# A first stage that loads six tiles of x first and builds its edge tables inside the loop over node tiles

## The chip, the core and the metric

The kernel runs on one core of one Trainium2 chip. The metric is the device time of one execution in microseconds (us). A core has TensorE (PE; its weight loads are shown as PEld), VectorE (DVE), ScalarE (ACT), GpSimd (POOL) and SyncE (SP), and 16 DMA engines that serve the queues of SP, ACT and POOL.

## The reference, cut to what matters

Two rounds of a relational graph layer and a mixture-of-experts layer, with 6250 nodes of 256 features and 100000 edges that are sorted by destination. The change touches only what feeds the first graph layer:

```python
x = x + _L0_gnn_ref(_layernorm(x, axis=-1), L0_gnn_W, L0_gnn_attn_src, L0_gnn_attn_dst, edge_index, edge_type_8)
...
h_all = jnp.einsum('nf,rof->rno', x, W).reshape(r, n, h, d)
src, dst = (edge_index[0], edge_index[1])
h_src = h_all[edge_type, src]
h_dst = h_all[edge_type, dst]
scores = jnp.einsum('ehd,hd->eh', h_src, attn_src) + jnp.einsum('ehd,hd->eh', h_dst, attn_dst)
```

Each node's normalised features are multiplied by 8 relation matrices of 256 x 256 and by the attention vectors folded into them. What follows reads one projected row for each edge.

## The kernel before, in words

The program is a sequence of stages with a barrier between them. The first, `relation_rows` (stage name `rows`), does three things.

**The loop over node tiles.** 6250 nodes are 49 tiles of 128. For each tile VectorE normalises (`Norm.normalise`, L228), TensorE transposes two blocks into PSUM (`Norm.transpose`, L236), ScalarE copies them to SBUF (`Norm.keep`, L265), TensorE multiplies by the 8 matrices (`product`, L643, into four PSUM banks in turn) and by the 64 columns for the destination half (L648), ScalarE copies the 8 results into one of two buffers `hb` (L470), VectorE copies the destination half (`half`, L543), and SP stores the buffer to `h_tab` in HBM (L424). VectorE normalises two tiles ahead; its order in the loop is normalise t+2, copy half t, then whatever table work is put behind tile t (`turns_at`). So what it does behind tile t stands ahead of the normalisation of tile t+3, which TensorE transposes after product t+1.

**What must come before the loop.** The matrices `wn` are loaded (SP, L405) and transposed by 32 matmuls (L616), ScalarE copies them (L451), and 64 small matmuls multiply them by the attention vectors (L623), which sit word by word in `ablk` (16 DMAs, L411). The mean and variance of all 49 tiles are made by `tile_stats` (L201, four quarters of x as ACT's queue loads them, L447 and L448) and `statistics`; ScalarE takes one square root of all variances (`root`, L222), for which it loads a table.

**The tables of edges.** Edges are cut into groups of 256 that never cross a block of 128 destination nodes. The destination of the first edge of each run of 128 (781 words, L401) is stored to HBM and loaded to 49 partitions (L407); VectorE counts positions (L492), GpSimd gathers a window of 256 edges for each block (L361), VectorE counts the cuts and groups (L504 to L510), TensorE makes prefix sums and spreads them (L628, L630), VectorE finds for each group its block, first edge and length (L520 to L533), and GpSimd gathers the rows and destinations of all groups, 8 indirect DMAs (L365, L367). The rest of it (`turn0` to `turn3`, `keep`, `turn5`, GpSimd's masks) already runs inside the loop, behind tiles 4 to 30.

The order of the work is written out by hand: each engine's program is a list, and semaphores tie them. The tables of edges stand ahead of the loop in VectorE's and TensorE's lists, and between the first and the second quarter of the statistics. SP waits in its list for the list of first edges (`first_st`) ahead of the attention vectors, and for the group table (`at_ok`) ahead of the loop's stores.

```python
            pe.wait_ge(consts, 1)
            pe.wait_ge(weights, 16 * 17)
...
            pe.wait_ge(need_ok, 1)
...
            turns_at = {4: turn0, 6: turn1, 8: turn2, 10: turn3, 30: turn5}
```

## Time and profile before

| | us |
|---|---|
| median of 3 runs | 3263.57 |
| lowest and highest run | 3260.66, 3266.58 |
| the profiled execution's own time | 3259.22 |
| its span, first to last instruction | 3257.2 |
| PE busy | 2189.7 (67% of the span) |
| DVE, ACT, POOL busy | 1780.9, 1332.3, 1589.4 |

The profile is one execution, taken by the hardware profiler. "Busy" counts the time in which an engine has an instruction under way; matmuls are pipelined, so a busy PE is not PE at its peak. PEclk is the granted TensorE clock as a share of full speed: 1.00 is 2.4 GHz, 0.50 is 1.2 GHz. SPq and ACTq are the issues of DMAs by SP and ACT; the duration of such a row is the time that the issuing engine spent on it, not that of the transfer. A releaser in brackets is what ended the idle time before an instruction.

### The profile page before, as it was taken

The page shows a single profiled execution, that of the slowest core. Times are in us where ns is not written, and L with a number is a line of the kernel's source. Part 1 is how long each engine was busy: PE and PEld are TensorE (multiplying, and loading weights), DVE is VectorE, ACT ScalarE, POOL GpSimd, SP SyncE. Part 2 cuts the span into 40 slices and gives each one's busy share as a digit, 9 for nine tenths or more (in the row PEclk, how much of TensorE's full clock was granted, in tenths as well). Part 3 has the DMA queues.
Part 4 walks back from the last instruction along what each step waited for, and adds up shares of the span by engine and source line. Part 5 has one row for each costly group of instructions (what it writes and reads, how often), then busy time and mean ns, then how long its engine had stood idle before and what let it go on. Part 6 is the DMA issues. An engine that isn't in the chain of part 4 may idle for free. (4 is left out here: it accounts for less than half of the span.)

```text
span 3257.2 us, 51141 instructions
## 1 busy us (share of the span) xinstructions
PE 2189.7 (67%) x13091; PEld 1849.9 (57%) x13092; DVE 1780.9 (55%) x4102; ACT 1332.3 (41%) x2969; POOL 1589.4 (49%) x1585
## 2 busy tenths in 40 slices
PE   2999985777777777777626085350430079999998
PEld 1888874656666556565426074230430069999997
DVE  4111125777777777776675434426663365656564
ACT  0444444655565655555301053130111344444443
POOL 1056217777777777777250534327227223334333
PEclk8999986888888888888755588685555589999999
DMA  6355447777765555556542244222302632222221
GB/s 141 126 208 213 193 172 210 214 209 211 208 194 144 145 145 145 144 144 132 53 123 72 78 158 144 68 74 51 97 31 104 210 77 42 46 48 47 48 47 26
DMA packets 225887, 402.34 MB, mean 124 GB/s; under 512 B 58684, under 2 KB 153543, under 8 KB 219086
## 3 DMA queue, kind: packets, MB, share of 16 engines
q0 software_dynamic: 84864, 206.63, 26.2%
q1 hardware_dynamic: 122002, 187.73, 17.3%
q10 hardware_dynamic: 18892, 6.45, 0.9%
q8 instruction: 57, 0.93, 0.1%
q14 instruction: 72, 0.59, 0.1%
HBM read 247.26 MB, written 155.68 MB: 124 GB/s over the span
## 5 line engine op out<-in xcount | busy, mean ns | idle before, releaser
L720 POOL DMA_INDIRECT sum_ring<-h_tab,gnn_edge_row x880 | 839.4, 954 | 268.0 <-issue 260.7
L981 PE MATMUL sum_bank<-sum_ring,sum_one_hot 128*128 128x264 f32 x1760 | 583.0, 494 | 215.2 <-issue 195.7
L981 PEld LDWEIGHTS sum_bank<-sum_ring,sum_one_hot 128*128 128x128 f32 x1760 | 418.7, 247 | 334.5 <-issue 227.0
L1802 POOL DMA_INDIRECT out_dram<-moe_y,moe_to_node x112 | 185.9, 1659 | 383.9 <-ACT moe_y L1828 353.0
L643 PE MATMUL rows_bank<-rows_w_rows,rows_xnT 128*128 128x264 f32 x1568 | 358.6, 387 | 1.7 <-ACT rows_xnT L265 1.7
L643 PEld LDWEIGHTS rows_bank<-rows_w_rows,rows_xnT 128*128 128x128 f32 x1568 | 295.1, 191 | 50.3 <-ACT rows_xnT L265 2.1
L770 ACT ACTIVATE sum_distance_by_lane<-all_iota,gnn_minus_local 128x128 bf16<-128x128 f32 x880 | 267.3, 386 | 0.1
L836 DVE TENSOR_TENSOR sum_ring<-sum_ring,sum_bank 128x1024 f32<-128x1024 f32 x220 | 265.7, 1209 | 0.5 <-ACT sum_ring L784 0.4
L970 PEld LDWEIGHTS sum_bank<-gnn_dst_half,sum_one_hot_T 128*128 128x128 f32 x1760 | 226.2, 205 | 43.9 <-issue 40.3
L970 PE MATMUL sum_bank<-gnn_dst_half,sum_one_hot_T 128*128 x1760 | 230.9, 289 | 28.7 <-ACT sum_one_hot_T L763 14.3
L1960 PE MATMUL moe_bank<-moe_w_low,moe_hidden_high 128*128 x896 | 244.2, 273 | 0.0
L1960 PE MATMUL moe_bank<-moe_w_high,moe_hidden_high 128*128 x896 | 244.2, 273 | 0.0
L1960 PE MATMUL moe_bank<-moe_w_high,moe_hidden_low 128*128 x896 | 244.2, 273 | 0.0
L470 ACT ACTIVATE rows_h_rows<-rows_bank 128x264 f32<-128x264 f32 x392 | 152.9, 390 | 198.5 <-PE rows_bank L643 198.5
L843 DVE TENSOR_TENSOR nodes_acc<-sum_bank,nodes_acc 128x264 f32 x440 | 188.2, 428 | 47.7 <-PE sum_bank L981 19.3
L1844 ACT ACTIVATE moe_hidden<-moe_bank,moe_b_T 128x256 f32<-128x256 f32 x456 | 186.3, 475 | 42.8 <-PE moe_bank L1950 25.5
L543 DVE COPY gnn_dst_half<-rows_bank 128x64 f32<-128x64 f32 x49 | 11.0, 225 | 332.1 <-PE rows_bank L648 332.1
L775 ACT ACTIVATE sum_one_hot<-sum_distance_by_lane,all_ones 128x1024 f32<-128x1024 bf16 x110 | 126.3, 1148 | 147.4 <-PE sum_bank L981 145.5
L1950 PE MATMUL moe_bank<-moe_x_high,moe_w_high 128*128 128x256 f16 x912 | 175.3, 274 | 1.7 <-DVE moe_x_low L1894 1.7
L1950 PE MATMUL moe_bank<-moe_x_low,moe_w_high 128*128 128x256 f16 x912 | 175.3, 274 | 0.0
L1950 PE MATMUL moe_bank<-moe_x_high,moe_w_low 128*128 128x256 f16 x912 | 175.1, 274 | 0.0
L826 DVE TENSOR_TENSOR sum_score<-sum_dst_part,sum_ring 128x64 f32<-128x64 f32 x110 | 24.9, 226 | 266.6 <-DMA sum_ring<-h_tab,gnn_edge_row 266.0
(406 smaller groups left out, 4151.3 us busy)
## 6 DMA issues: line engine op xcount, KB each, us to landing
h_tab<-rows_h_rows SPq DMA_DIRECT2D x49, 1056.0 KB, 3.9
sum_local_rows<-local_tab SPq DMA_DIRECT2D x110, 256.0 KB, 3.8
sorted<-sum_blank_row SPq DMA_DIRECT2D x49, 387.0 KB
moe_stage<-in_L_ffn_W_dram SPq DMA_DIRECT2D x16, 1024.0 KB
moe_tile<-sorted POOLq DMA_DIRECT2D x58, 258.0 KB, 4.1
sum_ring<-h_tab,gnn_edge_row POOLq DMA_INDIRECT x880
sorted<-sum_zero SPq DMA_DIRECT2D x49, 256.0 KB
mask_tab<-rows_masks POOLq DMA_DIRECT2D x7, 1560.0 KB, 7.9
```

The source lines that it names most:

```text
L470: nc.scalar.activation(hb[:, t % 2, r, :], bank[2 + r % 4][:, 0:W0], ACT.Copy).then_inc(h_ok.sem, 1)
L643: last = nc.tensor.matmul(bank[2 + r % 4][:, 0:W0], norm.xT[:, u, c * P:(c + 1) * P], wx[:, c, r, :], start=(c == 0), stop=(c == DC - 1))
L720: nc.gpsimd.indirect_dma_start(ring[:, t % (RING * ST), :], None, k.h_tab, bass.IndirectOffsetOnAxis(k.edge_row[:, t:t + 1], 0)).then_inc( ...
L770: last = nc.scalar.activation(off[:, u * P:(u + 1) * P], k.iota[:, :], ACT.Abs, bias=k.minus_local[:, m * ST + u:m * ST + u + 1])
L836: nc.vector.tensor_tensor(to, to, by, ALU.mult).then_inc(msg_ok, 1)
L843: nc.vector.tensor_tensor(col(k.acc, b), sum_b[g % SG][:, 0:W0], col(k.acc, b), ALU.add).then_inc(added, 1)
L970: last = nc.tensor.matmul(pick_b[n % 2][:, u * R * H0:(u + 1) * R * H0], hotT[:, n % 2, u, :], col(k.dst_half, b[u // G]), start=True, sto ...
L981: last = nc.tensor.matmul(sum_b[j][:, 0:W0], hot[:, m % 2, t, :], ring[:, m % RING * ST + t, :], start=(u == 0), stop=(u == G - 1))
L1802: nc.gpsimd.indirect_dma_start(a["out"], bass.IndirectOffsetOnAxis(to_node[:, n % 2, h:h + 1], 0), y[:, n % 2, h, :], None, bounds_check=N ...
L1844: last = nc.scalar.activation(hg[:, q, m * B1:(m + 1) * B1], bank[q][:, m * B1:(m + 1) * B1], ACT.Gelu, scale=1.0 / (XS * WS), bias=col(b1 ...
L1950: last = nc.tensor.matmul(bank[q][:, m * B1:(m + 1) * B1], w1[pw][:, c, bass.ds(e * F1 + (2 * q + m) * P, P)], xh[px][:, u, c, :], start=( ...
L1960: last = nc.tensor.matmul(bank[6 + u][:, h * D:(h + 1) * D], hh[ph][:, u, m, h * P:(h + 1) * P], w2[pw][:, m, bass.ds(e * D, D)], start=(m ...
```

## The change

It rewrites the first stage's order and leaves every other stage alone.

- **Loads.** SP issues the 8 source vectors, the matrices in two halves, tiles 6 to 17 of x, the 781 first words, the edge columns, then behind the wait for the words the rest of x. ACT issues the 8 destination vectors and tiles 0 to 5 of x. TensorE waits for each half of the matrices on its own, and for the vectors only ahead of the small matmuls.
- **Statistics in four parts** of 6, 12, 15 and 16 tiles: the first ahead of the loop, the others inside (`stats`, `variance`, `scales`; ScalarE's `root` ahead of tiles 3, 10 and 16). `tile_stats` had a loop in the instruction stream, `stats` is written out.
- **The tables of edges** become functions that VectorE runs behind tiles 1, 2, 3, 5 and 7; the two matmuls stand behind tiles 4 and 6; `turn0` to `turn3` move from tiles 4, 6, 8, 10 to 9, 11, 13, 15, the transposed arrays from 13 to 18, `turn5` from 30 to 32, and SP's stores and loads of tables with them.
- **First edges of each node.** Two loads to 128 partitions, one word a time, on ACT's queue ahead of the loop, become two loads of rows on SP behind tile 4, a cast, two transposes on TensorE behind tile 27 and two copies.

```diff
-        NF, TURN0 = E // P, 13
+        NF, TURN0 = E // P, 18
...
+        weights = [s.sem(f"weights_loaded{j}") for j in range(2)]
+        quarter = [0, 6, 18, 33, NT]
...
+            vectors(sp, 0, "L0_gnn_attn_src")
+            for j in range(2):
+                sp.dma_start(wn[:, j * R // 2:(j + 1) * R // 2], a["L0_gnn_W"][j * R // 2:(j + 1) * R // 2].rearrange("r (c p) f -> p r c f", p=P)).then_inc(weights[j], 16)
...
+                load_x(1)
                 sp.dma_start(k.first_s.rearrange("(t o) -> t o", o=1), a["dst"][0:NF * P].rearrange("(t p) -> t p", p=P)[:, 0:1]).then_inc(first_st, 16)
+                sp.dma_start(e_row[:, :], a["src"].rearrange("(p e) -> p e", p=EP)).then_inc(edges, 16)
+                sp.dma_start(e_type[:, :], a["edge_type_8"].rearrange("(p e) -> p e", p=EP)).then_inc(edges, 16)
+                sp.dma_start(line(k.dst_s[0:E]), line(a["dst"])).then_inc(line_st, 16)
...
                 sp.wait_ge(first_st, 16)
                 sp.dma_start(first[:, :], line(k.first_s).broadcast_to([NT, NF])).then_inc(first_in, 16)
...
+                load_x(2)
+                load_x(3)
...
                 for t in range(NT):
                     sp.wait_ge(h_ok.sem, 8 * t + 8 + 4)
                     sp.dma_start(rows(k.h_tab.rearrange("(n r) o -> n (r o)", r=R), t * P, P), flat(hb[:, t % 2, :, :])).then_inc(stored.sems[t % 2], 16)
-                    if t == 11:
+                    if t == 1:
+                        sp.wait_ge(rows_ok, 1)
+                        sp.dma_start(k.row_s[0:E].rearrange("(p e) -> p e", p=EP), e_row[:, :]).then_inc(line_st, 16)
...
+            vectors(act, 1, "L0_gnn_attn_dst")
+            act.dma_start(k.x[:, 0:quarter[1], :], a["x"][0:quarter[1] * P, :].rearrange("(t p) f -> p t f", p=P)).then_inc(loaded[0], 16)
...
-            norm.root(act)
+            root(0)
+            norm.t_ok.start(act)
...
+                if t in (3, 10, 16):
+                    root((3, 10, 16).index(t) + 1)
...
+            stats(0)
+            variance(0)
+            scales(0)
...
-            turns_at = {4: turn0, 6: turn1, 8: turn2, 10: turn3, 30: turn5}
+            turns_at = {1: edge_rows, 2: positions, 3: cuts, 5: block_lines, 7: groups, 9: turn0, 11: turn1, 13: turn2, 15: turn3, 26: first_edges, 28: keep_first, 32: turn5}
+            stats_at = {0: (stats, 1), 1: (variance, 1), 3: (scales, 1), 6: (stats, 2), 8: (variance, 2), 10: (scales, 2),
+                        12: (stats, 3), 14: (variance, 3), 16: (scales, 3)}
...
+                if t in stats_at:
+                    stage, j = stats_at[t]
+                    stage(j)
                 if t in turns_at:
                     turns_at[t]()
...
-            pe.wait_ge(weights, 16 * 17)
             for r in range(R):
+                if r % 4 == 0:
+                    pe.wait_ge(weights[r // 4], 16)
...
+            pe.wait_ge(attn_in, 16 * 2 * H0)
...
+                if t == 4:
+                    pe.wait_ge(need_ok, 1)
+                    nc.tensor.matmul(bank[7][0:NT, 0:1], k.before[0:NT, 0:NT], need[:, :], start=True, stop=True).then_inc(start_ps, 1)
```

The order of SP's DMAs up to the first stores of the loop, before:

```order
L397 DMA rows_edge_rows<-in_src_dram 125x800
L398 DMA rows_edge_type<-in_edge_type_dram 125x800
L399 DMA dst_line<-in_dst_dram 16x6250
L401 DMA first_dst<-in_dst_dram 781x1
L403 DMA row_line<-rows_line_end_i 1x512
L404 DMA dst_line<-rows_line_end_i 1x512
L405 DMA rows_w_natural<-in_L_gnn_W_dram 128x16x256
L407 DMA rows_first_dst<-first_dst 49x781
L411 DMA rows_attn_blocks<-in_L_gnn_attn_src_dram 32x1 x8
L411 DMA rows_attn_blocks<-in_L_gnn_attn_dst_dram 32x1 x8
```

and now:

```order
L355 DMA rows_attn_blocks<-in_L_gnn_attn_src_dram 32x1 x8
L415 DMA rows_w_natural<-in_L_gnn_W_dram 128x8x256 x2
L412 DMA nodes_acc<-in_x_dram 128x12x256
L418 DMA first_dst<-in_dst_dram 781x1
L419 DMA rows_edge_rows<-in_src_dram 125x800
L420 DMA rows_edge_type<-in_edge_type_dram 125x800
L421 DMA dst_line<-in_dst_dram 16x6250
L423 DMA row_line<-rows_line_end_i 1x512
L424 DMA dst_line<-rows_line_end_i 1x512
L426 DMA rows_first_dst<-first_dst 49x781
L412 DMA nodes_acc<-in_x_dram 128x15x256 x2
L430 DMA nodes_acc<-in_x_dram 106x256
```

The weights moved ahead of the edges, and 43 tiles of x (`nodes_acc`) stand on SP, 31 of them behind the load of the first words.

VectorE behind tiles 7, 8 and 9 (L596 is the copy of the destination half, L228 the normalisation of a tile to come), now:

```order
L596 COPY gnn_dst_half<-rows_bank 128x64
L562 TENSOR_SCALAR rows_group<-all_col 128x1 x4
L564 COPY rows_block_lines<-rows_bank 128x147
...
L575 CAST rows_edge_of_group<-rows_of_group 128x4
L228 TENSOR_SCALAR rows_xn<-nodes_acc,rows_mean,rows_rstd 128x256
...
L596 COPY gnn_dst_half<-rows_bank 128x64
L601 TENSOR_SCALAR rows_valid<-rows_lane,rows_of_group 128x256 x4
L602 CAST rows_to_turn<-rows_group_rows 128x1024
L228 TENSOR_SCALAR rows_xn<-nodes_acc,rows_mean,rows_rstd 128x256
```

The first use of the gathered groups (L602) stands two tiles behind the table that the gathers need (L575), and ahead of a tile's normalisation.

ScalarE between the weights and the loop, now:

```order
L476 ACTIVATE rows_w_rows<-rows_bank 128x8x8
L477 ACTIVATE rows_w_dst<-rows_bank 128x64
L481 ACT_TABLE_LOAD
L481 ACTIVATE rows_sd<-rows_var 128x6
L265 ACTIVATE rows_xnT<-rows_bank 128x256 x2
```

The table load and the square root, of 6 columns now, still stand behind the copies of the folded vectors; the two word-by-word loads that stood between square root and L265 are gone.

## Rows read from the trace of the kernel before

**Rows 1.** Busy us by stretch: PE, PEld, DVE, ACT, POOL; PEclk, DMA share, GB/s.
```profile
0.00:82.00 82.00, 16.50 (x104) 15.63 (x105) 36.31 (x131) 8.06 (x17) 15.25 (x23) 0.81 0.61 140
82.00:466.00 384.00, 383.13 (x1882) 331.64 (x1882) 50.49 (x131) 171.52 (x441) 117.95 (x77) 1.00 0.47 177
```

**Rows 2.** Stores of projected rows, whole trace; durations, first and last start.
```profile
L424 SPq DMA_DIRECT2D h_tab<-rows_h_rows x49: 319/320/349, 91.5 to 465.5; - x49
```

**Rows 3.** Time line, 55 to 92 us: start, us, engine, line, operation [idle before].
```profile
55.36 0.15 DVE L520 TENSOR_SCALAR rows_group<-all_col 128x1 f32<-128x1 f32 x1 [0.15 <-DVE rows_diagonal L517]
...
61.47 0.17 DVE L533 CAST rows_edge_of_group<-rows_of_group 128x4 int32<-128x4 f32 x1
...
77.06 0.24 ACT L222 ACTIVATE rows_sd<-rows_var 128x49 f32<-128x49 f32 x1 [21.58 <-DVEq L213]
...
79.01 0.74 DVE L228 TENSOR_SCALAR rows_xn<-nodes_acc,rows_mean,rows_rstd 128x256 f32<-128x256 f32 x2 [0.25 <-DVE rows_rstd L286]
...
81.86 0.66 ACT L265 ACTIVATE rows_xnT<-rows_bank 128x256 f32<-128x256 f32 x2 [4.56 <-issue]
...
82.30 8.79 PE L643 MATMUL rows_bank<-rows_w_rows,rows_xnT 128*128 128x264 f32 x32 [1.70 <-ACT rows_xnT L265]
...
91.54 7.29 PE L643 MATMUL rows_bank<-rows_w_rows,rows_xnT 128*128 128x264 f32 x32
```

**Rows 4.** Time line of 39 to 56 us.
```profile
39.30 6.07 PE L616 MATMUL rows_bank<-all_ident,rows_w_natural 128*128 128x128 f32 x32 [39.30 <-DMA rows_attn_blocks<-in_L_gnn_attn_dst_dram]
...
45.21 8.36 PE L623 MATMUL rows_bank<-rows_attn_blocks,rows_w_natural 128*128 128x16 f32 x64
...
54.20 1.28 ACT L222 ACT_TABLE_LOAD   x1
...
55.32 0.85 PE L630 MATMUL rows_bank<-rows_diagonal,all_ones 49*128 49x147 f32 x2 [1.49 <-DVEq L518]
```

**Rows 5.** Time line of the first 40 us, DMA issues (SPq, ACTq).
```profile
1.29 28.13 ACTq L447 DMA_DIRECT2D nodes_acc<-in_x_dram  x4
...
10.64 0.42 SPq L405 DMA_DIRECT2D rows_w_natural<-in_L_gnn_W_dram  x1
...
22.37 1.30 SPq L407 DMA_DIRECT2D rows_first_dst<-first_dst  x1
23.71 4.12 SPq L411 DMA_DIRECT2D rows_attn_blocks<-in_L_gnn_attn_src_dram  x8
27.87 3.79 SPq L411 DMA_DIRECT2D rows_attn_blocks<-in_L_gnn_attn_dst_dram  x8
29.45 9.93 ACTq L448 DMA_DIRECT2D nodes_acc<-in_x_dram  x1
```

**Rows 6.** Busy time by stretch; last two columns: busy share of DMA, GB/s.
```profile
10.00:20.00 10.00, 0.00 (x0) 0.00 (x0) 1.28 (x3) 0.00 (x0) 0.00 (x0) 1.00 0.84 162
20.00:30.00 10.00, 0.00 (x0) 0.00 (x0) 0.00 (x0) 0.00 (x0) 0.00 (x0) 1.00 1.08 352
```

**Rows 7.** Time line, VectorE and the last mask store of GpSimd.
```profile
62.11 4.01 DVE L201 BATCH_NORM_STATS2 nodes_stats<-nodes_acc  x12 [0.47 <-DVE rows_edge_of_group L533]
...
122.61 1.13 DVE L548 TENSOR_SCALAR rows_valid<-rows_lane,rows_of_group 128x256 f32<-128x256 f32 x4
...
124.38 0.41 DVE L228 TENSOR_SCALAR rows_xn<-nodes_acc,rows_mean,rows_rstd 128x256 f32<-128x256 f32 x1
...
353.30 0.84 POOL L391 DMA_DIRECT2D mask_tab<-rows_masks  x1 [0.30 <-POOL rows_masks L389]
```

**Rows 8.** Busy time by stretch, behind the group gathers.
```profile
74.00:76.00 2.00, 0.00 (x0) 0.00 (x0) 1.87 (x7) 0.00 (x0) 0.00 (x0) 0.50 0.58 204
76.00:78.00 2.00, 0.00 (x0) 0.00 (x0) 1.49 (x6) 0.24 (x1) 0.00 (x0) 0.50 0.00 0
```

**Rows 9.** Busy time by stretch, in the small matmuls; PEclk is third from last.
```profile
50.00:51.00 1.00, 1.00 (x11) 1.00 (x10) 0.29 (x2) 0.00 (x0) 0.00 (x0) 1.00 0.09 16
52.00:53.00 1.00, 1.00 (x7) 1.00 (x6) 0.00 (x0) 0.00 (x0) 0.00 (x0) 0.50 0.00 0
```

More of the change, by code:

```diff
@@ L344, in relation_rows, with vectors @@
         block = s.block()
+        def vectors(eng, j, name):
+            eng.wait_ge(cleared, 1)
+            with nc.allow_non_contiguous_dma(reason="attention vectors, one word a lane"):
+                for h in range(H0):
+                    p0 = h * HD0 % P
+                    eng.dma_start(ablk[p0:p0 + HD0, h * HD0 // P, j * H0 + h:j * H0 + h + 1],
+                                  a[name][h:h + 1, :].rearrange("a b -> b a")).then_inc(attn_in, 16)
         @block.gpsimd
@@ L456, in _, with root @@
                 nc.scalar.activation(wd[:, c, :].rearrange("p (r h) -> p r h", r=R), got_v[:, c, :, 1, :], ACT.Copy).then_inc(v_ok, 1)
-            norm.root(act)
+            def root(j):
+                part = slice(quarter[j], quarter[j + 1])
+                act.wait_ge(norm.var_ok, j + 1)
+                nc.scalar.activation(norm.sd[:, part], norm.var[:, part], ACT.Sqrt).then_inc(norm.sd_ok, 1)
+            root(0)
+            norm.t_ok.start(act)
             h_ok.start(act)
-            with nc.allow_non_contiguous_dma(reason="the first edges, one word a node"):
-                for t, name in ((k.dst_i, "dst"), (k.src_i, "src")):
-                    act.dma_start(t[:, :], a[name][0:NPAD].rearrange("(t p) -> p t", p=P)).then_inc(first_nodes, 16)
             norm.keep(act, 0, 0, d_ps)
             for t in range(NT):
+                if t in (3, 10, 16):
+                    root((3, 10, 16).index(t) + 1)
                 if t + 1 < NT:
@@ L533, in _, with variance @@
-            ch.link(nc.vector.tensor_copy(at_i[:, :], got[:, 1, :]))
-            v.sem_inc(at_ok, 1)
-            for j in range(1, 4):
-                stats(j)
-            norm.statistics(v, ch)
+                for t in range(quarter[j], quarter[j + 1]):
+                    last = nc.vector.bn_stats(k.stats[:, t, :], k.x[:, t, :])
+                ch.link(last)
+            def variance(j):
+                part = slice(quarter[j], quarter[j + 1])
+                moments(nc, ch, *(k.stats[:, part, i] for i in (1, 2, 4, 5)), norm.mean[:, part], norm.var[:, part], norm.tmp[:, part])
+                v.sem_inc(norm.var_ok, 1)
@@ L539, in _ @@
+            norm.xn_ok.start(v)
             d_ok.start(v)
@@ L625, in _ @@
             last.then_inc(v_ps, 1)
-            pe.wait_ge(need_ok, 1)
-            nc.tensor.matmul(bank[7][0:NT, 0:1], k.before[0:NT, 0:NT], need[:, :], start=True, stop=True).then_inc(start_ps, 1)
-            pe.wait_ge(diag_ok, 1)
-            nc.tensor.matmul(bank[7][:, 8:8 + 3 * NT], k.ones[0:NT, :], diag[:, :, :].rearrange("p j b -> p (j b)"), start=True, stop=True).then_inc(lines_ps, 1)
             pe.wait_ge(v_ok, 4)
```

163 lines of the change are left out of this document (93 added, 70 removed).

## The prediction

> **What bounds the kernel now.** First the busy time by stretch, for the first stage alone [rows 1]: in the 384 us from 82 to 466 the matmul engine is busy for 383.13 us at a granted clock of 1.00, while in the 82 us before it does 16.50 us of work. The stage is therefore a long stretch that only the matmuls set, behind a preparation in which TensorE mostly waits. The stores of the projected rows give the pace of the loop: 49 of them from 91.5 to 465.5 [rows 2], so 374.0 / 48 = 7.79 us a tile. A change that makes no product cheaper can gain only by letting the first product start earlier than 82.30 [rows 3], and loses whatever it makes TensorE wait inside the loop. The next stage starts after the last store has landed, so a shift of the loop passes through to the end.
>
> Then the time line, read backwards from 82.30 [rows 3]. The first product waits for ScalarE to copy a transposed tile at 81.86; the tile was normalised from 79.01, after the square root at 77.06, after the statistics of all 49 tiles, which come behind the edge and block tables (group table from 55.36 to 61.64). Nothing of tables or of tiles 6 to 48 is needed for product 0. TensorE's own preparation ran from 39.30 to 53.57 [rows 4], and began at 39.30 because the attention vectors, issued from 23.71 to 31.7 behind a wait for the little list of first edges (22.37), landed last [rows 5]. The weights were issued only at 10.64.
>
> **The change, part by part.** I rebuild the time of product 0.
>
> *Loads.* ACT's first load, behind the same memsets, was issued at 1.29. Eight vector DMAs now stand on SP and eight on ACT, at once; sixteen took 4.12 + 3.79 us of issue [rows 5], so eight end near 5.2. The two weight halves (1.05 MB each) and the six tiles of x (0.79 MB) are issued by 6.0. I let their data flow from about 7.0, an estimate of 1 to 2 us behind the issue. The rows offer two rates: 352 GB/s where only long rows move, and 162 GB/s where the 781 single words and the edge columns move too [rows 6]. I take 352, since the single words now stand behind weights and x on their queue. First weight half with x: 1.84 MB / 352 GB/s = 5.2 us, at hand near 13. Both halves: 2.89 MB, 8.2 us, near 16. At 162 GB/s the second half would come near 25: that is the upper bound.
>
> The Trainium skill (DMA: Bandwidth & Descriptors, section "Issuing engines are not separate DMA queues") says that transfers issued by different engines run on the same 16 DMA engines and interleave, so that a second issuer saves only issue time. By it the x load on ACT delays the weights, as I have counted; with queues of their own the first half would need 3.0 us instead of 5.2 and TensorE could start 2.2 us earlier, though the second half would bind then.
>
> *Weights on TensorE.* The 32 transposes take 6.07 us, the 64 small matmuls 8.36 us [rows 4]. They start at 13, the second half's 3 us start at 16 or later, the small ones at 19.1 and end at 27.5. At 25 for the second half it would be 36.5.
>
> *From there to product 0.* ScalarE empties the vectors (53.57 to 54.20), and then loads the table for the square root, 1.28 us [rows 4]; the new order keeps that load behind the four copies. Then 0.05, then from square root to normalised tile 79.01 - 77.06 = 1.95, and about 1.5 for the first transposes, the copy and the product's start, against 3.3 before (82.30 - 79.01): the two word-by-word loads that kept ScalarE from its copy until 81.86, an idle time "issue" of 4.56 us, are gone [rows 3]. Sum: 0.63 + 1.28 + 0.05 + 1.95 + 1.5 = 5.4, so product 0 at 32.9. The six-tile statistics (half of the 4.01 us of twelve [rows 7], and seven short operations) are done by 18 and hide behind the weights. **Gain: 82.3 - 32.9 = 49.4 us.**
>
> *What enters the loop.* VectorE has two short instructions a tile. What it does after product t must end, with the next normalised tile, before product t+1 ends. Six of the 49 tiles have a group of transposes more, so I take 7.74 us for an ordinary one, just under the mean of 7.79; less 0.4 for the normalised tile and 0.2 for the copy, 7.1 us are left. The slots: statistics of 12, 15, 16 tiles at 0.335 a tile [rows 7], 4.0, 5.0 and 5.4; group table 55.36 to 61.64 less a gap of 0.3 [rows 3], 6.0; the other slots issue fewer or shorter instructions than these. All fit, the group table with some 1.1 us to spare. Cost nothing; were the budget exceeded, each us would be paid in full.
>
> *A wait that is new.* The group table (slot 7) lets GpSimd issue eight gathers, one per 1.25 us. Before, they followed at once and the traffic they caused ran until about 76, 15 us after the table's end at 61.64, and was zero after [rows 3, 8]; the first use was at 122.61 [rows 7]. Now the use is in slot 9, 15.5 us after slot 7 begins, that is 9.2 us after the table is ready. VectorE waits 5.7 us there, works 1.8 us (122.61 to 124.38) and normalises in 0.4 [rows 7]: ready 23.4 us after slot 7, where TensorE needs the tile after 23.2. Bounds: nothing, or 4 us if the stores of rows (1 MB a tile) slow the gathers. I take 1.7 us. Queued behind that wait on VectorE are tile 12's normalisation and with it every product from 11 on.
>
> *TensorE's own extras.* The two table matmuls (0.85 us for the second with both its passes [rows 4]) and two small transposes now stand between products: 1.0 us, bounds 0.6 and 1.5.
>
> *SP.* Its queue now holds, behind the first x and weights: 12 tiles of x, the single words, edges, a wait for the words, the last 31 tiles of x, and only then the stores of the loop. I put the words at 26, x issues until about 40, the loop's first store (due at 42) on time. Nothing charged; see the first rival.
>
> *Hidden.* The node tables leave after tile 16 instead of 11, from a start 49 us earlier: about 10 us earlier in all. GpSimd issued its last mask table at 353.30 [rows 7], so the masks end some 75 us before the loop does.
>
> Sum: 49.4 - 1.7 - 1.0 = **46.7 us**. The profiled execution took 3259.22 (span 3257.2 and 2.0 around it) and becomes 3212.5. It lies 4.35 us below the median of the runs, 3263.57, from which I get **3217 us**.
>
> **The rivals.** *The stores come late.* Two tiles of rows can wait unstored; the third blocks ScalarE, then TensorE. For it: issuing the x loads occupied ACT's queue for 28.13 us for four and 9.93 for the tail, and SP's wait for the list of first edges ended at 22.37 [rows 5]. With the words at 28, 11 us for each of two loads of 15 tiles (three loads of 12 took 27.7) and 9.9 for the tail, SP enters the loop at 60. It may be as late as 46 without harm, so it costs 14 us: 3231. Against it: before, the tail of x was issued by 39.4 although edges, weights and x all shared that time, and the bytes are the same.
>
> *The gathers or a slot stall more.* Gathers 4 us later and the window wait in slot 3 late by 2: 3217 + 5 = 3222.
>
> *The weights' work runs at the low clock.* The granted clock is 1.00 from the start of the trace with TensorE idle, and fell to 0.50 (1.2 GHz) at 51, in the small matmuls: 11 a us before, 7 after [rows 9]. Were 0.50 granted from the beginning, 14.4 us would become up to 22.7: 3225 at most, I say 3223. The Trainium skill (TensorE: Matmul & The Clock Gate, section "What's actually happening") calls the throttled clock the default that activity lifts, which would give this rival; the 1.00 beside an idle engine speaks against it here, so it gets little.
>
> *Slower than before: the clock stays low in the loop.* The first tile took 91.54 - 82.30 = 9.2 us instead of 7.74 [rows 3]. By 11 against 7 matmuls a us [rows 9], a tile wholly at the low level costs 7.74 * 4 / 7 = 4.4 us more. From eleven such tiles on the gain is gone; twenty make 3217 + 88 = 3305. For it: the clock fell while TensorE was busy with small matmuls, and a stall in slot 9 gives new idleness. Against it: the mean clock of 1.00 over 384 us of loop.
>
> *The front does not move.* If some early wait still held product 0 near 80, the time would be 3264 within a few us; no wait in the new order reaches that far, since table and full statistics stand behind product 0.
>
> **How the numbers follow.** The forecast, 3209 to 3225, has 0.62; late stores (3225 to 3245) 0.17; larger slot stalls 0.07; low clock in the preparation 0.07; nothing gained 0.03; slower 0.04. 3209 is the forecast without a stall, without the drop of clock (2 us) and with the 3 us by which the runs shown spread; 3233 takes in the slow weights (+9), both smaller rivals and most of the late stores. A measurement of this kernel tells about 0.2%, 6.5 us, from no change: faster by more 0.94, within 0.02, slower 0.04.
>
> **What would show it.** Product 0 near 33, behind the square root's table load; weights at hand near 16; a store every 7.7 us from about 42; one wait of VectorE for the gathers in slot 9 of 5 to 6 us with 1 to 2 us of idle TensorE; the next stage starting near 424. A first store later than 46, idle TensorE in tiles 2 or 3, or a low granted clock after the first tile would make it wrong.

## The result, and the profile of the changed kernel

| us | before | changed |
|---|---|---|
| median (4 runs each) | 3265.07 | 3239.38 |
| lowest and highest | 3260.66, 3267.99 | 3233.63, 3241.23 |
| profiled execution, its span | 3259.22, 3257.2 | 3241.23, 3239.6 |
| stores of the loop, first and last | 91.5, 465.5 | 48.5, 428.8 |
| first instruction of the second stage | 470.6 | 433.9 |

The ratio is 0.9917, with a 95% interval of 0.9901 to 0.9933: 25.7 us faster by the medians, where 46.7 were predicted, and outside the range. The busy time by stretch, as in [rows 1]:

```profile
0.00:32.00 32.00, 15.12 (x100) 14.85 (x101) 9.03 (x28) 7.86 (x17) 5.46 (x13) 0.86 0.80 192
32.00:434.00 402.00, 389.46 (x1890) 335.13 (x1888) 85.28 (x275) 171.66 (x444) 127.89 (x88) 0.98 0.51 185
```

The 82 us of preparation became 32. The second stretch runs to 434, 5.2 us past the last store at 428.8, while that of [rows 1] ends 0.5 us past it. Between the same two marks, the first product and the last store, the loop takes 396.5 us (32.28 to 428.8) where it took 383.2 (82.30 to 465.5): 13.3 us longer. TensorE is idle for 7.3 us of that, where it was idle for 0.1, and its mean clock is 0.99. The time line of the first 33 us answers to [rows 3 to 5]:

```profile
1.03 3.65 SPq L355 DMA_DIRECT2D rows_attn_blocks<-in_L_gnn_attn_src_dram  x8
...
4.73 1.05 SPq L415 DMA_DIRECT2D rows_w_natural<-in_L_gnn_W_dram  x2
...
13.01 5.22 PE L675 MATMUL rows_bank<-all_ident,rows_w_natural 128*128 128x128 f32 x32 [13.01 <-DMA rows_w_natural<-in_L_gnn_W_dram]
...
18.07 9.18 PE L683 MATMUL rows_bank<-rows_attn_blocks,rows_w_natural 128*128 128x16 f32 x64
...
27.87 1.28 ACT L481 ACT_TABLE_LOAD   x1
...
32.28 1.25 PE L699 MATMUL rows_bank<-rows_w_rows,rows_xnT 128*128 128x264 f32 x2
```

Product 0 (the matmuls of tile 0) starts at 32.28. Sixteen matmuls later TensorE stops. The same view from 33 to 49 us:

```profile
35.63 3.86 SPq L430 DMA_DIRECT2D nodes_acc<-in_x_dram  x1
39.53 2.47 SPq L432 DMA_DIRECT2D node_tab<-rows_row_zero  x1
42.09 1.24 ACT L495 ACTIVATE rows_h_rows<-rows_bank 128x264 f32<-128x264 f32 x4 [9.44 <-SPq L90]
...
42.54 5.51 PE L699 MATMUL rows_bank<-rows_w_rows,rows_xnT 128*128 128x264 f32 x16 [4.29 <-ACT rows_h_rows L495]
...
48.51 0.36 SPq L436 DMA_DIRECT2D h_tab<-rows_h_rows  x1
```

The releaser of ScalarE's first copy of a result is `SPq L90`, a semaphore increment in SP's own list: `stored.start(sp)`, which declares both row buffers free. It stands behind all of SP's loads, and SP came out of them at 42.0. With all four PSUM banks full TensorE waited, and its granted clock fell back (0.50 from 44 to 46). Before, the first store left 9.24 us behind the start of product 0 (82.30 to 91.54), which would be 41.5 here. It left at 48.51: **7.0 us**.

The second place is tiles 8 to 10:

```profile
111.69 0.44 SPq L442 DMA_DIRECT2D block_tab<-rows_block_of_group  x1
...
119.06 3.73 PE L699 MATMUL rows_bank<-rows_w_rows,rows_xnT 128*128 128x264 f32 x16
...
124.59 1.24 ACT L495 ACTIVATE rows_h_rows<-rows_bank 128x264 f32<-128x264 f32 x4 [4.95 <-DMA h_tab<-rows_h_rows]
...
129.34 1.14 DVE L601 TENSOR_SCALAR rows_valid<-rows_lane,rows_of_group 128x256 f32<-128x256 f32 x4 [10.07 <-DMA rows_group_dst<-dst_line,rows_edge_of_group]
...
131.86 2.39 PE L699 MATMUL rows_bank<-rows_w_rows,rows_xnT 128*128 128x264 f32 x10
```

Product 10 took from 119.06 to 131.86, 12.8 us instead of 7.74. VectorE waited 10.07 us for the gathers, not 5.7; but before that ScalarE waited 4.95 us for a store of rows to land. Of the stores' landing times (median 3.9 us) the longest is 13.2, that of tile 8. The wait that ended last is VectorE's, by 0.64 us of idle TensorE ahead of the next tile's transposes (131.59); without ScalarE's, VectorE's alone would have held product 11 as long. What runs there (busy by stretch; the last two columns are the DMA engines' busy share and GB/s):

```profile
114.00:116.00 2.00, 2.00 (x11) 1.71 (x10) 0.00 (x0) 0.81 (x3) 1.70 (x2) 1.00 1.37 273
116.00:118.00 2.00, 2.00 (x10) 1.71 (x9) 0.00 (x0) 1.00 (x3) 1.39 (x3) 1.00 0.69 29
...
120.00:122.00 2.00, 2.00 (x11) 1.71 (x10) 0.00 (x0) 0.00 (x0) 0.00 (x0) 1.00 1.03 37
...
126.00:128.00 2.00, 2.00 (x6) 1.46 (x6) 0.00 (x0) 0.39 (x1) 0.00 (x0) 0.50 1.04 437
```

The engines are mostly busy for a share of 0.7 to 1 and move 29 to 37 GB/s, while the store of the 512 single words of `block_tab` is under way (issued at 111.69, landed at 124.8). It is not the words that fill the time: in the trace's records of DMA packets 510 of them take 8 ns each, between 114 and 116. It is the gathers' packets of some 4 KB behind them, which take 1.5 us each (mean) from 116 to 124, and 0.25 us with the stores' from 124 to 128. The Trainium skill (DMA: Bandwidth & Descriptors, section "Specifications") names 512 B as the least transfer for full rate, and says that below it the engine reads, modifies and writes. The trace agrees that such a store is dear, 2 KB in 13.1 us; how it comes about, and why it holds up others, no run here shows. The kernel before has the same stretch behind the same store, with nobody waiting in it, and the rows of the groups come only from 72 us, as in [rows 8]:

```profile
64.00:66.00 2.00, 0.00 (x0) 0.00 (x0) 2.00 (x7) 0.00 (x0) 1.39 (x3) 0.50 1.09 29
...
70.00:72.00 2.00, 0.00 (x0) 0.00 (x0) 1.65 (x6) 0.00 (x0) 1.41 (x2) 0.50 0.22 10
72.00:74.00 2.00, 0.00 (x0) 0.00 (x0) 2.00 (x7) 0.00 (x0) 0.00 (x0) 0.50 0.55 180
```

So the first stage gained 36.7 us (470.6 to 433.9). The span gained only 17.6. By the first instruction of each stage, later stages took in all 19.1 us more: 15.6 in the first expert stage, 2.7 in the second router stage, 0.8 in the rest.

### The profile page after: what moved, and what is told of

The parts are those of the page before. It is cut to its first block and busy times, and to the rows that moved or that the text cites. A ratio compares the mean times of both kernels' runs of the same rounds, so it can differ in the third digit from the quotient of the medians.

```text
span 3239.6 us, 51080 instructions
## 1 busy us (share of the span) xinstructions
PE 2211.0 (68%) x13093; PEld 1867.8 (58%) x13094; DVE 1787.7 (55%) x4141; ACT 1335.4 (41%) x2972; POOL 1590.5 (49%) x1585
## 5 line engine op out<-in xcount | busy, mean ns | idle before, releaser
L596 DVE COPY gnn_dst_half<-rows_bank 128x64 f32<-128x64 f32 x49 | 11.0, 225 | 295.3 <-PE rows_bank L704 295.3
```

## The experiments

Theories at the start. GATE: the late allowance costs 7 us. WORDS: the single words of the block table, beside gathers and stores, cost 3 to 5 us more than charged. They ran on four further chips. On two of them either kernel takes 10% to 12% longer, nearly all of it in the stage behind the first, so ratios and the first stage are compared, not levels; "like chips" are the other two. "Stage end" is the first instruction of the second stage. Each chip's own kernel before is the one that a ratio is taken against.

**The kernel again.** No edit.

> The changed kernel once more, unchanged. Its first trace lost 36.7 us in the first stage but only 17.6 in all, because the first expert layer (stage moe0) ran 30 us and 15 us of its loop at a granted clock of 0.50 and took 15.8 us longer. Theory CHANCE: the clock's drop there differs from execution to execution; this trace shows the stage at another length (by more than 3 us) and the first stage again 36 to 37 us shorter. Rival FIXED: the drop belongs to this kernel's timing, and this trace shows the same two stretches at 0.50 and the same 15 to 16 us.

3551.64 against 3597.67, ratio 0.9879 [0.9861, 0.9897]. ScalarE waited 6.46 us for SP, 3.2 for the store, VectorE 9.3 for the gathers; stage end 432.3. Product 0 was at 35.1 here, because the small matmuls took 11.1 us instead of 9.18, and the gate hid that: the first store left at 46.64, 2.3 us late by the 9.24 above, not 7.0. ScalarE's copies in the expert loop span 121.6 us instead of 133.6, so that length is not fixed to the kernel. But the whole expert stage took 406.1 us, within 1 us of the first trace's 405.3, which CHANCE had denied: its sign came in the loop alone.

**The allowance first.**

```diff
+            stored.start(sp)
             vectors(sp, 0, "L0_gnn_attn_src")
...
-                stored.start(sp)
                 for t in range(NT):
```

> One line moved: SP gives ScalarE the allowance for the two row buffers at the head of its program instead of behind all of its loads. Theory GATE: ScalarE's first copy waits at 32 to 42 us for that signal alone, not for a buffer; the copy comes at about 34, TensorE does not stop in product 0, the first store is at 41 to 42 instead of 48.5, and the first stage ends 6 to 8 us earlier (near 427); about 3232 us if the later stages keep their times. Rival LOADS: the x loads on SP's queue would hold the stores up anyway; the stall moves to tile 1 or 2 and less than 2 us is gained.

3548.42, ratio 0.9867 [0.9842, 0.9892]. Product 0 ran through (31.88 to 40.4); the first store left at 42.77, held 1.9 us by SP, which was in its issues until 42.7; stage end 426.6, 7.3 before the first trace of the changed kernel and 5.7 before the one on this chip. GATE holds in the traces; the median fell by 3.2 us only, within the spread of 5 and 6 runs.

**The block table's words later.**

```diff
-                    if t == 8:
+                    if t == 24:
                         sp.wait_ge(at_ok, 1)
...
-                    if t == 10:
+                    if t == 26:
                         sp.wait_ge(block_st, 16)
```

> SP's store of the block table (512 single words) and its reload move from behind tiles 8 and 10 to behind tiles 24 and 26; all else as changed. Theory WORDS: the single words hold up everything on the DMA engines. The gathers of the groups land by slot 9 plus 5 us (VectorE's wait 10.1 falls below 6), the store of tile 8 lands in under 6 us instead of 13.2, and the stall of 5 us moves from tile 10 to tile 26; the total stays within 3 us. Rival GATHERS: the eight gathers themselves are slow beside the row stores; wait and late store stay at tile 9 and 10, and nothing much happens at tile 26.

3540.56, ratio 0.9846 [0.9822, 0.987]. VectorE's wait fell to 4.63 us and ScalarE's 3.2 near tile 10 went; stage end 428.9, 3.4 us earlier. WORDS holds for the gathers and for tile 10. The stall that I expected to move with the words to tile 26 did not come (ScalarE waited for a store only near 309 and 333 us, 0.57 and 1.09 us), so that the total fell where I had it stay. In the records of DMA packets all 128 of the store ahead of the words were through at 242, and the next store, at 245.52, took 6.9 us to land, still before its buffer was needed. The sixth experiment shows that the words can hold a store without gathers beside them too.

**Both.**

> Both edits of the two runs before. GATE and WORDS together: first stage ends 6 to 8 us earlier than changed, about 427, with one stall near tile 26. GATE and GATHERS: the same end, with the stall at tile 10. If the later stages keep their times, 3232 us; but their clock may fall otherwise, and by CHANCE or by a shift of the stage's start the total may differ by up to 16 us from that.

3539.23, ratio 0.9842 [0.9824, 0.9861]; stage end 422.3, 10.0 before the changed kernel on this chip and 11.6 before its first trace. Its time line:

```profile
32.13 8.69 PE L699 MATMUL rows_bank<-rows_w_rows,rows_xnT 128*128 128x264 f32 x32
34.35 0.39 ACT L495 ACTIVATE rows_h_rows<-rows_bank 128x264 f32<-128x264 f32 x1 [1.85 <-PE rows_bank L699]
...
42.09 0.35 SPq L436 DMA_DIRECT2D h_tab<-rows_h_rows  x1
...
117.64 1.14 DVE L601 TENSOR_SCALAR rows_valid<-rows_lane,rows_of_group 128x256 f32<-128x256 f32 x4 [3.28 <-DMA rows_group_dst<-dst_line,rows_edge_of_group]
```

The two effects add (5.7 and 3.4 singly on this chip, 10.0 together), and are together the 10 us that the first stage missed.

**The kernel before again**, on a chip like the first:

> The kernel before, unchanged. Its ratio shows how far the measurement strays from 1. Its trace is read for the first expert stage (from the first to the last of ScalarE's copies behind the gate: 117.6 us in the first trace of the kernel before, 133.6 in that of the changed kernel, 121.6 to 129.8 in four traces of its variants, always with a granted clock that falls to 0.50 in places). Theory SHIFT (what is gained early is partly given back because the later stages begin at another moment or in another state): 117.6 within 1.5, granted clock 1.00 throughout, as in the first trace. Theory CHANCE (the clock in that stage falls in some executions of either kernel, and the two traces happened to differ): another value, 120 to 130, with a clock that falls in places. In either case the first stage ends at 470.6 within 3.

3266.57 against 3268.91, ratio 0.9994 [0.9979, 1.001]. Its stage end was 474.1 and its expert stage as in its first trace. That was SHIFT's forecast, but see the next ones.

**The tables ahead of the loop again**, with the new loads:

```diff
+            for part in (edge_rows, positions, cuts, block_lines, groups):
+                part()
             stats(0)
...
-            turns_at = {1: edge_rows, 2: positions, 3: cuts, 5: block_lines, 7: groups, 9: turn0, ...}
+            turns_at = {9: turn0, ...}
```

> The changed kernel with the tables of edges back ahead of the loop (the new order of loads, the first part of the statistics and everything else stay). It parts the gain in two. The first words are stored by 27.1, their load lands by 41, the windows are gathered behind SP's store of rows at 42 to 46, and the group table took 13.4 us from the windows' arrival (48.23 to 61.64), so it is ready near 62 to 65; the first part of the statistics, root and normalisation take 6 more: product 0 at 68 to 71 instead of 32. If both the loads and the tables hold the start, as the time line said, that is 12 to 14 us earlier than before's 82.30, and the tables' move is worth 36 to 39 us of start. SP's allowance is given before product 0 here, so no stop in tile 0, and slot 9 has no wait for gathers: loop from store 0 at 78 to 80, stage end at 458 to 462; time 10 to 12 us under before. A rival, that the loads alone would have done most of it (tables overlap with the wait for x): product 0 under 55, stage end under 445.

3264.23, ratio 0.9991 [0.9976, 1.0006], where I had 10 to 12 us; stage end 465.6. Product 0 at 73.68, later than I expected:

```profile
43.45 0.26 SPq L434 DMA_DIRECT2D row_line<-rows_edge_rows  x1
52.48 1.17 POOL L373 DMA_INDIRECT rows_window<-dst_line,rows_position_i  x1 [46.28 <-DMA row_line<-rows_edge_rows]
...
66.59 0.17 DVE L574 CAST rows_edge_of_group<-rows_of_group 128x4 int32<-128x4 f32 x1
...
73.68 8.45 PE L704 MATMUL rows_bank<-rows_w_rows,rows_xnT 128*128 128x264 f32 x32
```

I had let that store land in 3 us; issued at 43.45 behind x it took 9. The loads alone bring 8.6 us of start against the first trace of the kernel before (11.5 against the one on this chip), 8.5 us of stage end, and no time that can be told from none by the medians; the tables' move is worth 41 us of start. The kernel also shows the words by themselves. Its gathers were over by 80, the block table's store left at 144.85, and the store of rows that left 0.36 us before it still took 14.3 us to land:

```profile
158.80 1.24 ACT L494 ACTIVATE rows_h_rows<-rows_bank 128x264 f32<-128x264 f32 x4 [5.99 <-DMA h_tab<-rows_h_rows]
```

**The first tile made early.** Beside both cures: square root, and tile 0's transposes and copy, ahead of the folded vectors.

```diff
+            root(0)
+            norm.keep(act, 0, 0, d_ps)
             act.wait_ge(v_ps, 1)
...
             for fc in range(DC):
+                if fc == 1:
+                    norm.transpose(pe, 0, 0)
```

> Both cures (allowance for the row buffers given first; table of blocks stored after tile 24), and: ScalarE takes the first square root with its table load, and TensorE and ScalarE make the first transposed tile, ahead of the folded vectors instead of behind them; SP issues the last 106 rows of x and the one-row store behind tiles 0 and 2. Theory HEAD (the 4.9 us between the end of the small matmuls and product 0, 27.2 to 32.1, are root, scales, normalisation and transposes in a row, none of which needs the folded vectors): product 0 at 28.0 to 28.8, first store at 36.5 to 38, stage end 4 us below 422.3, at 418 to 419.5; time 15 us under the changed kernel's. Rival QUEUE (SP is still in its issues of x until 36 to 40 and takes the gain back): product 0 as early, first store at 39 to 40 or later, a wait of ScalarE for the store in tile 2, stage end 420 to 422. Rival CLOCK (the transposes between the small matmuls let the clock fall earlier or keep it low in the first tile): the first products take 8.7 us and more, half the gain is gone.

3222.68, ratio 0.986 [0.9837, 0.9883], 6.6 us under the changed kernel beside it where HEAD had 15. Product 0 at 30.14, first store at 39.92, stage end 420.8. QUEUE's numbers came (a first store near 40, 1.0 us of ScalarE waiting for a store in tile 2, an end between 420 and 422), but not by its way: SP was out of its issues of x at 35.6, and the store left as product 0 ended. Both HEAD and CLOCK are in it, as TensorE's rows and the stretches show (PEclk third from last):

```profile
22.93 5.86 PE L689 MATMUL rows_bank<-rows_attn_blocks,rows_w_natural 128*128 128x16 f32 x32
...
30.14 9.32 PE L703 MATMUL rows_bank<-rows_w_rows,rows_xnT 128*128 128x264 f32 x32
```

```profile
22.00:24.00 2.00, 1.43 (x14) 1.35 (x13) 1.15 (x3) 0.39 (x1) 0.00 (x0) 1.00 0.68 90
24.00:26.00 2.00, 2.00 (x12) 2.00 (x12) 0.00 (x0) 0.00 (x0) 0.00 (x0) 0.50 0.50 70
```

The clock is at 0.50 from 25 to 34 in every trace with the new loads but the delayed one below, whether product 0 is at 30, at 35 or at 74. The small matmuls end at 28.8 instead of 27.1 (0.57 us of that is TensorE's idle time ahead of the interruption), tile 1's transposes still stand ahead of product 0, and more of product 0 lies in the low stretch (9.32 us for 8.69): of 4 us 2.0 are left at its start, and 2.2 at the first store. CLOCK was right in the effect; that the transposes lower the clock is not shown, since it fell at the same time without them.

**The changed kernel again**, beside it:

> The changed kernel, unchanged, beside the others. Under CHANCE its first expert stage lies anywhere between 117 and 134 us; under SHIFT it is above 121 again. Its first stage ends at 432 to 434, and its ratio is 0.988 to 0.992.

3229.28, ratio 0.9874 [0.9855, 0.9893], stage end 435.4, expert stage 390.7 us to the next stage. SHIFT in its plain form falls: the first stage was 38.7 us ahead of the kernel before on the same chip, and the span 43.0.

**One more pair, and a delay.**

> The kernel before, unchanged, for one more trace of its first expert stage (first to last instruction of the stage: 386.9 and 388.4 us in two traces of the kernel before; 402.6 and 388.0 in two of the changed kernel, 403.5 to 413.0 in four of its variants on a chip where the kernel before took 3598 us and was not traced). Theory CHIP (the length goes with the chip or with the execution, and either kernel has both): on a chip where the changed kernel shows over 400 this one does too. Rival KERNEL (only the changed kernel ever has over 400): 386 to 389 here whatever the changed kernel shows. The second router stage lasts 238.5 us to the next stage's first instruction, as in both traces of the kernel before.

> The changed kernel, unchanged, beside the delayed one. Under CHIP its first expert stage is within 3 us of that of the kernel before in this call; under KERNEL it may be 15 us longer. First stage ends at 432 to 436; second router stage 241.3 us as in every kernel with the change.

```diff
+            for j in range(8):
+                nc.gpsimd.memset(mask[:, :, :, :], 0.0).then_inc(lag, 1)
+                pool.wait_ge(lag, j + 1)
             nc.gpsimd.memset(ablk[:, :, :], 0.0).then_inc(cleared, 1)
```

> The changed kernel with 8 memsets of 2.7 us put ahead of GpSimd's first, for whose semaphore both queues' first loads wait, and all else behind them: the whole program 21.5 us later, nothing else. Theory PASS (a shift of the loop passes through to the end, as the prediction had it): median 21.5 us above the changed kernel's in this call, within 4, each later stage as long as there within its own scatter of about 2 us, first expert stage apart. Theory SHIFT (the later stages give part of a shift back because of when they start): the difference is under 16 or over 27, and a stage other than the first differs by 5 or more.

Before 3268.55 and expert stage 391.5; changed 3233.36, ratio 0.9877 [0.9851, 0.9903], 395.4; delayed 3260.78, ratio 0.9965 [0.995, 0.998], 396.0. The delay moved the stage end by 22.6 us (433.5 to 456.1) and the span by 21.3; no later stage differed by more than 2.3. By the medians it cost 27.4. That is 1.9 outside what PASS allowed and 0.4 inside SHIFT's "over 27", with intervals of 5 to 8 us on it; SHIFT's other sign, a later stage that differs by 5 us, did not come. So the traces speak for PASS, and the medians can't decide.

**VectorE's list padded**, on the kernel with the early tile:

```diff
+            for _ in range(29):
+                ch.link(nc.vector.memset(lim[0:1, 0:1], 0.0))
             stats(0)
```

> The kernel with both cures and the early first tile, and 29 memsets of one word in VectorE's list ahead of the first statistics, where VectorE waits for x from 7 to 13 us. They lie in that wait (29 of 0.1 us at most) and cost nothing. Theory PLACE (the second router stage is 2.9 us longer in every kernel with the change because VectorE's list is 3 instructions longer ahead of it, so that its loop's instructions lie elsewhere in the stream, and each turn of the loop takes 2.71 instead of 2.57 us): with 29 more the loop is shifted by 32 against the kernel before, a multiple of any small block of instructions, and the stage is back at 238.5, a turn at 2.57. Rival STATE (something of the change that lives on in memory or queues makes the stage longer): 241.3 as before. First stage as with the early first tile, end at 420 to 422; time 8 to 15 us under the changed kernel's.

3223.22, ratio 0.9854 [0.9831, 0.9878], stage end 420.8. The second router stage took 238.9 us, against 241.2 to 241.5 in the six other traces of kernels with the change on such chips and 238.5 to 238.7 in three of the kernel before: PLACE holds, in that 29 instructions ahead of the loop and nothing else bring the time back. VectorE's rows in its loop, in the kernel before, the changed one and the padded one:

```profile
2346.42 0.41 DVE L228 TENSOR_SCALAR route_xn<-nodes_acc,route_mean,route_rstd 128x256 f32 x1 [0.43 <-PE route_bank L236]
...
2349.00 0.41 DVE L228 TENSOR_SCALAR route_xn<-nodes_acc,route_mean,route_rstd 128x256 f32 x1 [0.43 <-PE route_bank L236]
```

```profile
2310.02 0.41 DVE L228 TENSOR_SCALAR route_xn<-nodes_acc,route_mean,route_rstd 128x256 f32 x1 [0.56 <-PE route_bank L236]
...
2312.73 0.41 DVE L228 TENSOR_SCALAR route_xn<-nodes_acc,route_mean,route_rstd 128x256 f32 x1 [0.56 <-PE route_bank L236]
```

```profile
2301.93 0.41 DVE L228 TENSOR_SCALAR route_xn<-nodes_acc,route_mean,route_rstd 128x256 f32 x1 [0.46 <-PE route_bank L236]
...
2304.53 0.41 DVE L228 TENSOR_SCALAR route_xn<-nodes_acc,route_mean,route_rstd 128x256 f32 x1 [0.46 <-PE route_bank L236]
```

A turn of two tiles takes 2.58, 2.71 and 2.60 us, with the same instructions in it. Over the whole loop the median turn is 2.57 us in all five traces of the kernel before, 2.71 in the twelve others with the change, whatever the chip, and 2.61 in the padded one. That VectorE's list ahead of the loop had become 3 instructions longer was my count, and no trace shows it; the traces show that VectorE ran 39 more ahead of it (2872 for 2833), and 29 more again when padded. So the place in the list is shown to matter, and which places are good is not.

**The expert stage: two traces of each kernel, in turn.**

> The kernel before, unchanged: one more trace. Theory EXECUTION (when the granted clock rises in the expert loop, and whether it falls again inside it, differs from execution to execution of either kernel): among the traces of the kernel before in this call some first expert stage is 394 us or longer from its first instruction to the next stage's, where three traces so far had 389.6, 391.0 and 391.5. Rival KERNEL (only the changed kernel does it): all stay within 389 to 392.

> The changed kernel, unchanged: one more trace (so far 405.2, 390.7 and 395.4 us for that stage, 396.0 delayed). Both theories: between 389 and 406. Under KERNEL most of its traces lie above 392, under EXECUTION it has the same spread as the kernel before.

> As for the other trace of the kernel before in this call: 394 or longer in one of them under EXECUTION, 389 to 392 in all under KERNEL.

> As for the other trace of the changed kernel in this call: 389 to 406 under both; above 392 in most under KERNEL.

On this chip, one of the two with the longer second stage, the kernel before took 3663.28 and 3662.21 us, ratios 0.9964 [0.994, 0.9988] and 0.9965 [0.9923, 1.0008] against 3673.13 of the same kernel, and the changed one, with two runs each, 3622.14 and 3626.72, ratios 0.9849 [0.9755, 0.9943] and 0.9861 [0.9737, 0.9985]. The expert stage of the kernel before had 411.4 and 410.1 us, that of the changed one 405.4 and 411.0. The kernel before has long ones too, so KERNEL falls as it was put. That both pairs are long speaks for the chip as much as for the execution; but one kernel's traces on the first chip and the two like it had 405.2, 390.7 and 395.4. The stretches of the expert loop, in the first trace of the kernel before, in the first of the changed one, and in that long one of the kernel before:

```profile
1890.00:1910.00 20.00, 18.42 (x120) 15.63 (x121) 8.88 (x28) 11.50 (x41) 7.36 (x14) 0.98 0.55 174
1910.00:1930.00 20.00, 18.42 (x134) 16.09 (x133) 8.52 (x29) 11.80 (x42) 6.77 (x13) 1.00 0.58 189
```

```profile
1855.00:1875.00 20.00, 18.95 (x110) 16.46 (x110) 7.45 (x24) 11.05 (x38) 6.89 (x13) 0.84 0.52 162
1875.00:1895.00 20.00, 19.73 (x76) 16.65 (x75) 5.19 (x16) 7.80 (x24) 4.50 (x9) 0.54 0.33 107
...
1955.00:1975.00 20.00, 19.32 (x94) 16.77 (x93) 5.96 (x20) 9.31 (x32) 4.97 (x10) 0.66 0.40 132
```

```profile
2276.00:2296.00 20.00, 19.73 (x96) 17.43 (x96) 5.98 (x20) 8.55 (x28) 4.31 (x8) 0.64 0.36 114
```

In this loop TensorE is busy for 90% and more and sets the pace. Ahead of it the granted clock is 0.50 in every trace, and rises to 1.00 as the loop begins or up to some 30 us into it; here it also fell again twice, to a mean of 0.54 and 0.66 in the stretches shown. At the low level some 76 matmuls fit into 20 us instead of 120 to 134. Such a second fall inside the loop is in four of the thirteen traces with the change (the first one, the second and fourth experiment, one of the last pair) and in none of the five of the kernel before. That is too few to say whether the change has a part in it, and no experiment tests it.

## Why the prediction was wrong, step by step

- **Loads and weights: right.** Weights at hand at 13.0 and the second half at 16.1, in time; the transposes took 5.22 us instead of 6.07, the small matmuls 9.18 instead of 8.36. Product 0 at 32.28 for 32.9. The upper bound of 25 for the second half played no part. In three of the six traces of the changed kernel product 0 came 3 us later (see the rival on the weights below).
- **"SP. ... the loop's first store (due at 42) on time. Nothing charged": failed, +7.0 us.** The time at which SP comes out of its loads of x (about 40, and 39.5 in the trace) was estimated rightly; the one-row store behind them, 2.47 us, was not counted. It was judged harmless because two tiles of rows could wait unstored. But ScalarE may not write even the first of them before SP has given the allowance, so SP's limit was the first copy at about 34, not 46. The rival *the stores come late* named the right queue, but let SP enter the loop at 60 where it was 42, and had this same limit wrong. The allowance is an instruction in SP's list and moved with it: it stood behind the waits of SP's list before, too, and was never late there only because product 0 was at 82.30. The second experiment shows it. The price goes with product 0: by the first store 7.0 to 7.6 us in the three traces of the changed kernel where product 0 is at 32, 2.3 to 2.5 in the three where it is at 35.
- **"A wait that is new", 1.7 us: mis-sized, it was 5.1.** The prediction's own rows gave 0.2 (the tile ready at 23.4, needed at 23.2), and the rest was margin. I read the gathers' 15 us of traffic behind the table in [rows 3, 8] as theirs alone; for ten of them the block table's words were under way (61.73 to 71.7), which hold up the gathers' packets and a store of rows. Without the words beside it (third experiment) the wait was 4.63 us and product 10 took 8.4 us, 0.65 too many. I had counted that store of 512 words nowhere, though it stands in the new kernel behind a tile of its own. The third, fourth and sixth experiment show it.
- **Slots, extras of TensorE, hidden work: right.** Statistics 4.00 and 4.98, group table 6.0, TensorE's two table matmuls without a wait. What is left of the loop's 13.3 us behind the two stalls is 1.2 us, for the 1.0 of TensorE's extras.
- **"So a shift of the loop passes through to the end": right in the mechanism by the delayed kernel's trace, 19.1 us off in the sum.** Two things moved behind it: 2.7 us in the second router stage through the place of a loop in VectorE's list, whose turn is longer in every unpadded trace with the change; and the clock in the first expert stage, which differed by 15.6 us between the two first traces and by 14.5 between traces of the same kernel on like chips.
- The sum in the traces: 50.0 of start (82.30 to 32.28), less 7.0 for the allowance, less 5.1 in product 10, less 1.2 of extras is the measured 36.7; less 2.7, less 15.6, less 0.8 is 17.6. By the medians 25.7 were gained. That the other runs on that chip lost some 8 us less to the clock would fit, and is not shown, since only one run of each kernel there has a trace. On two like chips the gain was 39.6 and 37.0 us, on the other two 46 and more, and why the first chip gave 26 stays open beyond this: the clock in the expert stage took it in its one trace, and I can't say why it did so more often there. Where the clock took least, on the like chips, the gain is the first stage's, short of the forecast by the allowance and the words.
- ***The weights' work runs at the low clock*: argued away on a misreading, and it came in part.** The prediction says that the granted clock is 1.00 from the start beside an idle TensorE. In fact the traces hold no record of it before 16.2 us (44.2 in the kernel before); the views print 1.00 where there is none. TensorE's own pace tells the level, in the stretches of the changed kernel (first numbers behind the comma: busy us and number of matmuls):

```profile
14.00:15.00 1.00, 1.00 (x7) 1.00 (x6) 1.00 (x4) 0.61 (x2) 0.00 (x0) 1.00 1.09 345
15.00:16.00 1.00, 1.00 (x6) 1.00 (x5) 0.90 (x5) 0.74 (x2) 0.00 (x0) 1.00 1.09 359
16.00:17.00 1.00, 1.00 (x11) 1.00 (x10) 0.72 (x5) 0.92 (x2) 0.00 (x0) 1.00 1.09 359
23.00:24.00 1.00, 1.00 (x7) 1.00 (x6) 0.00 (x0) 0.00 (x0) 0.00 (x0) 0.50 0.13 54
```

  The 32 transposes run at 6 to 7 a us up to 16 and at 11 to 12 from there, the same two paces as in [rows 9]. In all 18 traces the pace changes so with the first record, 3 to 6 us behind TensorE's first matmul. So TensorE begins at the low level in both kernels, and the 6.07 us of [rows 4] had that in it already. How much of TensorE's work on the weights falls between rise and fall differs: its 64 small matmuls took 8.4 to 11.4 us over the traces of both kernels. In three of the six traces of the changed kernel they took 11.0 to 11.4, and product 0 was at 35.1 to 35.5.
- *Clock stays low in the loop*, *the front does not move*: neither came. In the loop the clock was down for a few us behind each of the two stalls, and part of their price. The range's lower end, 3209, adds up to 3210 by its own terms.

## What to carry to other kernels

When a list is reordered, look through it for instructions that are no work: an allowance for buffers, a semaphore that a wait elsewhere counts on. They move with the list, and their limit is the first use of the buffer, not the first reuse. A table that leaves as 512 single words was under way for 10 to 15 us here though it is 2 KB, and held up what was under way beside it: put it where neither a gather nor a store is awaited, or turn it into rows first (that second way was not tried). And an early part may be held by two things: the loads' order alone gave 8.6 us of start and no time that the medians show, with the tables moved as well 50. And ask whether a view has a record behind a number: a clock of 1.00 beside an idle engine was none.

## What was unexpected of the hardware

- A store of 512 words of 4 bytes to HBM lands after 10 to 15 us. Its own packets take 8 ns each; the packets of 4 KB of gathers beside it take 1.5 us each instead of 0.25 until it lands. The store of projected rows issued 0.4 us ahead of it landed after 13.2 to 15.1 us instead of 3.9 (14.3 without gathers), but after 4.5 and 4.8 in two kernels with the words behind tile 24; what decides is not shown.
- The same loop with the same instructions took 2.57 or 2.71 us a turn according to its place in VectorE's list; 29 one-word memsets far ahead brought it back to 2.61.
- Traces of one kernel on like chips differ by 14.5 us in a stage in which TensorE is busy for 90 to 95% of the loop, by when the granted clock rises to 1.00 there and whether it stays.
- The granted clock fell from 1.00 to 0.50 in the matmuls of 16 columns, with TensorE busy throughout: at 23.0 us in the first trace of the changed kernel, at 21 to 25 in the others but the delayed one (44), at 48 to 51 in the kernel before.
